# A transformer block on one core: inverting the softmax sums later, and the statistics of the next sequences earlier

## The reference

```
mod = (silu(c) @ wmod).reshape(4, 6, 1, 256)          # shifts, scales, gates
h = layernorm(x) * (1 + ca) + sa
qkv = h @ W_qkv.T + b_qkv                             # 16 heads of 16
scores = einsum('bhqd,bhkd->bhqk', Q, K) / 4
attn = softmax(scores + causal)                       # exp, divided by the row's sum
x = x + ga * ((attn @ V) @ W_o.T + b_o)
h = layernorm(x) * (1 + cb) + sb
top 2 of 8 experts per token, softmax over the two
x = x + gb * sum_e combine[e] * (silu(h @ w1[e]) @ w2[e])
```

## Time and profile before

| | us |
|---|---|
| median of three runs (lowest, highest) | 1002.97 (1001.2, 1007.18) |
| the profiled execution | 1007.08 |
| its span, from the first to the last instruction | 1005.0 |
| TensorE busy | 894.9 (89%) |
| VectorE busy | 724.2 (72%) |
| ScalarE busy | 582.1 (58%) |
| GpSimd busy | 355.6 (35%) |
| the eight reciprocals (line 1353), idle before them for their data | 2.7, in two of the eight |
| granted TensorE clock, mean | 0.968 of full speed |

### The profile page before, as it was taken

How to read it: one execution, slowest core, us unless ns; L and a number is a source line. 1 busy time by engine, 2 the same in 40 slices (tenths; PEclk the granted TensorE clock), 3 DMA queues, 4 the chain that set the end, 5 groups by cost and what they waited for, 6 DMA issues and landing times.

```text
span 1005.0 us, 19371 instructions
## 1 busy us (share of the span) xinstructions
PE 894.9 (89%) x6100; PEld 532.1 (53%) x6174; DVE 724.2 (72%) x2323; ACT 582.1 (58%) x1271; POOL 355.6 (35%) x311
## 2 busy tenths in 40 slices
PE   5788799998989999889999997879899999999990
PEld 3443335333444443453543452523698899999880
DVE  8788766879756789857688769799637584444488
ACT  3335475766486677676676857657535433343563
POOL 1422021233324113345013444014386465655530
PEclk7899899999999999999999999989999999999996
DMA  8446337236234366250653746205313323222699
GB/s 280 126 65 128 52 64 166 53 50 142 54 48 112 55 118 132 76 77 22 127 95 107 154 73 192 68 25 173 97 52 121 96 70 100 81 74 75 197 295 314
DMA packets 83235, 110.61 MB, mean 110 GB/s; under 512 B 15930, under 2 KB 56434, under 8 KB 83138
## 3 DMA queue, kind: packets, MB, share of 16 engines
q1 hardware_dynamic: 75506, 89.45, 38.7%
q0 software_dynamic: 6816, 18.62, 5.9%
q10 hardware_dynamic: 816, 1.32, 0.4%
HBM read 69.42 MB, written 35.41 MB: 104 GB/s over the span
## 4 chain that ended last, share of the span: by engine, by line
PE 63%; DVE 13%; ACT 10%; issue 6%; POOL 3%; DMA 3%; SPq 1%; another core or an unknown queue 0%; ACTq 0%; POOLq 0%; DVEq 0%
PE PO L1642 10%; PE PY L1519 10%; PE PH L1519 9%; PE PS L1622 8%; PE PM L1599 7%; ACT PR L1008 4%; PE PHT L1727 3%; PE PX L1654 2%; PE PX L1568 2%; DVE MXF L1321 2%; DVE JK L1318 2%; PE PS L1626 2%; ACT SF L991 2%; PE PX L1671 1%; PE PX L1577 1%
## 5 line engine op out<-in xcount | busy, mean ns | idle before, releaser
L1008 ACT ACTIVATE PR<-PS 128x512 f32<-128x512 f32 (+3 forms) x768 | 334.5, 497 | 149.7 <-PE PS L1626 113.0
L1318 DVE CUSTOM_DVE_ANT_0 JK<-PM,MK 128x128 bf16<-128x128 f32 (+3 forms) x512 | 239.5, 484 | 58.0 <-PE PM L1599 56.7
L1599 PE MATMUL PM<-QK 128*128 128x512 bf16 (+3 forms) x725 | 233.9, 330 | 25.5 <-DVE MXF L1321 14.7
L1622 PE MATMUL PS<-QK 128*128 128x512 bf16 (+3 forms) x737 | 236.6, 332 | 17.8 <-ACT PR L1008 12.7
L1321 DVE TENSOR_REDUCE MXF<-PM 128x1 f32<-128x512 f32 x256 | 175.2, 684 | 78.2 <-PE PM L1599 61.4
L1622 PEld LDWEIGHTS PS<-QK 128*128 128x128 bf16 x768 | 75.4, 99 | 177.6 <-ACT PR L1008 111.5
L1642 PE MATMUL PO<-PR,V 128*17 128x512 f32 (+3 forms) x1536 | 163.3, 498 | 0.1
L1599 PEld LDWEIGHTS PM<-QK 128*128 128x128 bf16 x768 | 75.7, 99 | 100.1 <-DVE MXF L1321 35.5
L1519 PE MATMUL PY<-W2S,HT 128*128 x852 | 119.7, 290 | 2.7 <-issue 1.8
L1626 PE MATMUL PS<-MT,identb 128*128 128x128 bf16 x512 | 112.3, 221 | 1.9 <-issue 1.0
L1519 PE MATMUL PH<-W1S,XT 128*128 x426 | 112.6, 400 | 0.8 <-DVE W2S L1473 0.8
(11 more groups left out here) (269 smaller groups left out, 1179.8 us busy)
## 6 DMA issues: line engine op xcount, KB each, us to landing
QK<-SD SPq DMA_DIRECT2D x180, 128.0 KB
SD<-SP SPq DMA_DIRECT2D x42, 256.0 KB, 2.9
OP<-OS SPq DMA_DIRECT2D x64, 64.0 KB
LP<-LR SPq DMA_DIRECT2D x64, 64.0 KB
W1S<-in_w SPq DMA_DIRECT2D x8, 512.0 KB, 6.1
X<-XA SPq DMA_DIRECT2D x3, 1024.0 KB, 8.2
H2D<-XA SPq DMA_DIRECT2D x3, 1024.0 KB, 4.9
YG<-YT SPq DMA_DIRECT2D x12, 256.0 KB
```

Source lines behind the costliest of these rows:

```text
L1008: eng.activation(PR[:, slot, i, c0:512], PS[m % 3][:, c0:512], ACT.Exp, scale=0.25).then_inc(S["exp"].sem, 1)
L1318: eng.tensor_tensor_reduce(JK[:, jk % 2, 0:w], PM[m % 3][:, 0:w], MK[:, 512 - w:512], 1.0, -3.0e38, ALU.add, ALU.max, MXA[:, mb, h, qt:qt ...
L1599: eng.matmul(PM[m % 3][:, 0:128 * (k1 - k0)], QK[:, r, h, 0, qt * 128:(qt + 1) * 128], QK[:, r, h, 1, k0 * 128:k1 * 128], start=True, stop ...
L1622: last = eng.matmul(PS[m % 3][:, c0:512], QK[:, r, h, 1, j * 128:(j + 1) * 128], QK[:, r, h, 0, 512 * f + c0:512 * f + 512], start=True, s ...
```

## The change

Two numbers in `schedule()`. The statistics and roots of sequences 2 and 3 are placed three steps sooner in their window (step 1 instead of 4). The reciprocal of pairs 0 to 6 is placed 5.5 steps behind its `lsum` instead of 4; since the delays of a list are counted from each other, `lrec` and `lrep` of that pair go 1.5 steps later as well. The step `div` has a place of its own and stays.

```diff
         if b > 1:
-            place(w - 1, 4, stats(b))
+            place(w - 1, 1, stats(b))
...
         if u < 2 * B - 1:
-            place(2 * u + 2, 7, [(0, ("lsum", u)), (4, ("recip", u)), (1, ("lrec", u)), (2, ("lrep", u))])
+            place(2 * u + 2, 7, [(0, ("lsum", u)), (5.5, ("recip", u)), (1, ("lrec", u)), (2, ("lrep", u))])
             place(2 * u + 2, 17, one("div", u))
```

## The result

Four runs of the changed kernel gave 1015.15 us in the median (1013.55 to 1018.71), beside 1002.73 (1001.2 to 1007.18, four runs) for the kernel before: ratio 1.0118, 95% interval 1.0094 to 1.0142. The forecast was 1003.6 us and, with a chance of 0.89, no change beyond half a percent. The kernel is 1.2% slower and the time lies outside the range of 999.3 to 1007.3.

A forecast was written before the change was run, and what follows sets the result against it. VectorE was taken as the bound in the stretches that matter, close with ScalarE and TensorE in one. Terms -0.7 - 0.4 + 0 + 1.7 = +0.6 us on the median 1002.97 gave 1003.6 us; range 999.3 to 1007.3.

The forecast's parts named there:

- The readings of order and waits: Expected signs: reciprocals not waiting, no root over 1.3 us, about four held roots, TensorE's wait at 674 about 4.5 us.
- Pair 1: Sequence 2's term: transfers release the division at 259.7 to 260.0 us, projection starts sooner; gain 0.7 us, bounds 0 and 2.5.
- sequence 3's: Pair 3's term: 1.7 us gained without the long root, 1.3 lost; net gain 0.4, bounds 2.0 gained, 1.1 lost.
- about half of it, 1.2 to 1.4 us, on TensorE: Sequence 3: VectorE's slack and three buffers let only this much of 2.4 us of held roots reach TensorE.
- Its gain: Sequence 3: without the 2.03 us stall TensorE's 1.34 us wait goes; 1.34 to 2.03 us gained, 1.7 taken.
- rival B: Pair 6's new wait also lowers TensorE's clock, its idle time growing to over 5 us; +2.7, 1005.7 us, chance 0.14.
- 4 x 0.6 = 2.4 us: Sequence 3: four roots each wait about 0.6 us on VectorE for a GpSimd multiplication to end.
- a fifth: Sequence 3: a possible further stall of about 0.6 us if the first two roots are held; left out of the sum.
- Pair 6: VectorE's own division: 0.5 us for the unhidden reciprocal, 1.2 for a new wait; cost 1.7, bounds 0.8 and 2.3.
- Pair 5 and the rest: Pair 5: worth 0, bounds 0.3 gained, 1.0 lost; pairs 0, 2 and 4: division up to 1.5 us later, 0.
- a state of the clock: Sign of being wrong: a time beyond 5 us either way means an unpriced state of clock or transfers.
- a clock loss of about 1: Whole kernel: allowance of about 1 us within the upper bounds, which sum to +5.4 us.

The follow-up runs named there:

- e14: Kernel before with sequence 3's roots two to a half step from their old place, statistics unmoved; ratio 0.9982.
- e13: Kernel before with sequence 3's statistics and roots three steps sooner, plus nine unread matmuls in TensorE's wait for the logits copy; ratio 1.0020.
- e9: Kernel before with sequence 2's statistics and roots three steps sooner and pair 1's reciprocal 1.5 steps later; ratio 1.0009.
- e7: Kernel before with the reciprocal of pair 6 alone 1.5 steps later; ratio 1.0021.
- e6: Kernel before with sequence 2's statistics and roots alone three steps sooner, reciprocals where they were; ratio 0.9963.
- e11: Kernel before with sequence 3's statistics and roots alone three steps sooner; ratio 1.0080.
- e15: The same kernel as e11 (sequence 3's statistics and roots alone three steps sooner than in the kernel before), measured again; ratio 1.0061.
- e8: Kernel before with sequence 3's eight statistics pairs three steps sooner, its roots left where they were; ratio 1.0024.
- e1: Kernel before with the first edit alone: statistics and roots of sequences 2 and 3 three steps sooner, reciprocals unmoved; 1008.94 us, ratio 1.0047.
- e4: Changed kernel with 14 unread matmuls on TensorE ahead of the projection's wait for the division in sequences 0, 1 and 2; 1019.86 us, ratio 1.0166.
- e5: Changed kernel with 14 unread matmuls on TensorE ahead of the projection's wait for the division in sequence 0 (pair 1) only; ratio 1.0106.

## Why the prediction was wrong

**The readings of order and waits held.** No reciprocal of pairs 0 to 6 waits for its data. Both roots of 2.16 and 2.19 us are gone. The transfer releases pair 1's division. Four roots of sequence 3 are held, of 0.82 to 1.21 us, within 400 to 411 us. Line 1357 waits for the replication, and TensorE's stop behind it has grown (to 3.9 us, not 4.5). Pair 1's division came 0.8 us or more later than forecast: 30.2 us behind mark 5.16, where 259.7 to 260 us are 29.1 to 29.4.

**The step that failed is sequence 3's**, "about half of it, 1.2 to 1.4 us, on TensorE": -0.4 us forecast, bounds -2.0 and +1.1, measured +7.0 to +7.2 us in five profiles of it and 1.0080 and 1.0061 in the times. Its gain was about right (1.7 forecast, 2.1 measured in e14). Its loss in lateness was too low: with the clock kept up (e13) it is 1.7 us behind the statistics, 2.7 behind the roots and 3.6 at piece 10.0, where I had counted 1.3 and at most 2.4. The slack behind the block absorbed none of it. The stretch so nets +1.4 us in e13, just beyond the bound. The largest part is missing from the sum altogether: 5.6 us of half speed in the traces, 4.0 of them at TensorE's new stop, 4.1 in the times. I had that mechanism, in rival B, but asked for it at pair 6 only, because there a wait of TensorE was already in the profile. I also misread that place: I wrote that the wait of 2.97 us brought none, but the clock fell 1.3 us behind the product at 673.93, where my rows ended at 674. At sequence 3 TensorE had not waited for the copy at line 1362 before, and I never asked which instruction stood behind the fourth held root. It was the one instruction that TensorE needed next.

**Held by how much.** I counted 4 x 0.6 = 2.4 us; it is 3.3 us, 0.7 to 1.05 us for each, the fourth the longest. The first two, which had not met a GpSimd instruction in the trace of the kernel before, are held too (0.98 and 0.82 us), but as two of the four, not as a fifth. They are scalar forms, which by the Trainium skill, "SBUF — State Buffer", section "Who interferes with whom", can take the ports shared with GpSimd; the trace agrees.

**Pair 1:** -0.7 forecast. With both edits at pair 1 alone (e9) the time is +0.9 us (-0.5 to +2.3), its stretch 55.3 us as before; in the changed kernel's profile +3.45. The term missed two things: from the start of the reciprocal to the division it took 8.8 to 9.5 us in the eight profiles with the later reciprocal of pair 1 (9.49 in the changed kernel) and not 8.56, and TensorE, coming early, stops for some 3 us or more, with half speed behind. It also missed that the early statistics do better without the later reciprocal: alone they gain 3.7 us.

**Pair 6:** +1.7 forecast (0.8 to 2.3), 2.1 measured (0.7 to 3.5). It held in the waits: VectorE waited 0.8 us for the replication (0.35 to 1.8 forecast), and from the last issue of the eight transfers to the division it took 1.78 us in the changed kernel and 1.73 in e7, as reckoned from pair 1, and not the 1.3 of the lower bound. That the size fits may be luck in part, since more half speed is in it.

**Pair 5 and the rest:** nothing that stands out of the spread between profiles. The parts add up: -3.7 (e6) + 4.6 (e9 less e6) + 2.1 (e7) + 8.0 or 6.1 (e11, e15) = 9.1 to 11.0 of 11.8 us.

**The chances.** Slower by over half a percent had 0.06. The last sentence of the prediction named "a state of the clock" not priced as what a time beyond 5 us would mean, but the range had only "a clock loss of about 1" for it.

**What stays open.** Why the half speed at the same stop of 3 us lasted 3.4 us in some profiles and 6.8 in others; why 10.2 us from 635.7 us on in the changed kernel, and from 622.2 on in e6, ran at half speed and in other profiles not; what brings the second spell behind sequence 3's stop. Pair 6 with its stop filled wasn't tried.

## What to carry to other kernels

Price a held instruction by what stands behind it in its queue and by who waits for that, not by the queue's slack: 3.3 us on an engine with room became 2 us of standstill on TensorE and 4 us or more lost to half speed. Where a change opens or lengthens a stop of TensorE (here 2.04 us, in e8 1.51), price the stretch behind it at half speed as well, and test that by giving TensorE work in the stop. Take apart edits that were made together: here one half of one of them gains 0.4%, and the rest costs 1.6%.

## What the runs showed of the hardware

The granted clock of TensorE fell at the stop of 2.04 us in all six profiles that have it unfilled (the changed kernel, e1, e4, e5, e11, e15), 0.6 to 1.3 us after the stop began, and stayed at 0.50 for 10.2 us in each, of which 8.8 to 9.5 us lie behind the stop, with TensorE busy nearly all the while; nine matmuls of 0.23 us in the stop kept it at 1.00. The Trainium skill, "TensorE: Matmul & The Clock Gate", section "Terms", puts the penalty at the time below full rate times the part of the clock that is missing: by it an estimate of 10.2 x (1 - 0.5) = 5.1 us for this spell, beside 4.0 us measured by the filling in the traces and 4.1 in the times; the part of the spell in which TensorE stood anyway can't cost anything. Over whole kernels it agrees: about 25, 14.1 and 11.5 us more at half speed for the changed kernel, e11 and e15, whose times grew by 12.4, 8.0 and 6.1. Among executions of one kernel less of it shows: over 29 of the kernel before, the time at half speed varies from 50 to 70 us, and the span grows by 0.27 us for each us of it. That TensorE is not the bound behind many of those spells would explain this, but isn't shown.

The same waits do not always bring the same clock. The kernel before, and then the changed one, behind waits of 1.47 and 0.55 us for ScalarE (the waits end at 439.84 and 440.89, and at 446.36 and 447.41):

```profile
438.00:442.00 4.00, 1.98 (x21) 1.03 (x20) 0.73 (x4) 3.95 (x9) 1.18 (x1) 1.00 1.10 135
442.00:446.00 4.00, 3.95 (x34) 2.31 (x33) 2.75 (x9) 3.69 (x10) 1.36 (x2) 1.00 1.13 136
```

```profile
444.00:448.00 4.00, 1.98 (x17) 1.15 (x18) 0.73 (x4) 4.00 (x9) 0.66 (x1) 0.99 1.08 146
448.00:452.00 4.00, 4.00 (x29) 2.51 (x32) 1.53 (x5) 2.96 (x7) 1.88 (x2) 0.58 0.99 131
```

TensorE was busy for 1.98 of 4 us in both, and only in one the clock fell. So one profile of each kernel can't price a stop, and the mean granted clock over many executions is the better witness.
